# Attention bias with a mask, added by accumulating DMAs instead of by GpSimd, in a three-stage decoder layer; another order of steps

## The reference

```
x = x + attn(ln(x))            # stage a: 8 heads of 128, one shared key/value head, causal
x = x + xattn(ln(x), ctx, bias, pad, mask)   # stage b: 16 heads of 16
x = x + ffn(ln(x))             # stage c: shared expert + 8 experts, top 2 by a gate

# xattn, per batch and head
scores = q @ k.T * scale + mask          # mask: [256, 256], one for all batches
scores = where(pad, -inf, scores)        # pad: [32, 256]
scores = scores + bias + bias            # bias: [32, 16, 256, 256], the one large input
out    = softmax(scores) @ v
```

## Time and profile before

| | us |
|---|---|
| median of 3 runs (2559.65 to 2561.14) | 2559.83 |
| profiled execution | 2559.14 |
| its span, first to last instruction | 2557.4 |
| busy in it: TensorE, ScalarE, VectorE, GpSimd | 2340.5, 2060.2, 2007.8, 1788.1 |
| granted TensorE clock, mean | 0.991 |
| DMA queues' packets, share of the 16 engines | 27.4% |

### The profile page before, as it was taken

The page is one execution under the profiler, slowest core; times in us unless marked ns, Lnnn a source line. Parts: engine busy times, 40 slices in busy tenths (PEclk is TensorE's granted clock), DMA queues, the critical chain, the costliest instruction groups (busy, mean ns, idle before and its releaser), DMA issues.

```text
span 2557.4 us, 77106 instructions
## 1 busy us (share of the span) xinstructions
PE 2340.5 (92%) x26176; PEld 2036.7 (80%) x26176; DVE 2007.8 (79%) x6672; ACT 2060.2 (81%) x6065; POOL 1788.1 (70%) x1899
## 2 busy tenths in 40 slices
PE   4789999999999999999999999999999999999987
PEld 3678888888888888888888888888888888888876
DVE  5578788778788778788778788778788778788765
ACT  6777888877888877888877888877889877889864
POOL 2566677866677866677866677866677766677764
PEclk9899999999999999999999999999999999999999
DMA  5232222232222232222232222232222232222230
GB/s 167 92 105 87 92 86 89 84 109 86 92 88 89 84 109 82 96 87 90 84 109 81 96 86 91 85 109 80 94 87 93 84 109 80 93 88 93 80 100 10
DMA packets 171126, 233.14 MB, mean 91 GB/s; under 512 B 20720, under 2 KB 119280, under 8 KB 170736
## 3 DMA queue, kind: packets, MB, share of 16 engines
q1 hardware_dynamic: 170736, 228.21, 27.4%
HBM read 202.98 MB, written 25.17 MB: 89 GB/s over the span
## 4 chain that ended last, share of the span: by engine, by line
PE 63%; DVE 13%; ACT 11%; issue 10%; POOL 3%; DMA 1%; SPq 0%; DVEq 0%; ACTq 0%; POOLq 0%
PE ps_c_out L955 10%; PE ps_c_hidden L955 10%; PE ps_a_misc L955 9%; PE ps_b_probsT L1083 8%; PE ps_b_misc L1097 3%; PE ps_b_misc L955 3%; PE ps_b_scores L1071 3%; PE ps_a_scores L1009 3%; PE ps_a_misc L1028 2%; DVE b_neg_scores L817 2%; POOL bias L510 2%; DVE a_qT L769 2%; PE ps_b_probsT L955 2%; PE ps_b_scores L955 2%; PE ps_a_probsT L1016 1%
## 5 line engine op out<-in xcount | busy, mean ns | idle before, releaser
L510 POOL TENSOR_TENSOR bias<-bias,b_mask 128x512 f32<-128x512 f32 x512 | 646.9, 1278 | 0.0
L817 DVE CUSTOM_DVE_ANT_0 b_neg_scores<-ps_b_scores,bias 128x256 f32<-128x256 f32 x1024 | 391.7, 419 | 95.3 <-PE ps_b_scores L1071 34.8
L531 POOL TENSOR_TENSOR c_hidden_lo<-c_hidden,c_hidden_hi 128x512 f16<-128x512 f32 x288 | 334.2, 1160 | 131.2 <-ACT c_hidden_hi L683 90.8
L825 DVE TENSOR_TENSOR b_probsT_lo<-ps_b_probsT,b_probsT_hi 128x512 f16<-128x512 f32 x512 | 352.7, 689 | 63.6 <-ACT b_probsT_hi L660 53.7
L1083 PE MATMUL ps_b_probsT<-constants,b_probs 128*128 128x128 f32 x2048 | 323.3, 281 | 29.1 <-DVE b_probsT_lo L825 15.1
L524 POOL TENSOR_TENSOR c_hidden<-c_relu 128x512 f32<-128x512 f32 x288 | 300.3, 1043 | 56.3 <-ACT c_relu L678 55.2
L660 ACT ACTIVATE b_probsT_hi<-ps_b_probsT 128x512 f16<-128x512 f32 x512 | 303.1, 592 | 24.8 <-PE ps_b_probsT L1083 20.0
L955 PE MATMUL ps_c_out<-w_hi,c_hidden_hi 128*128 128x256 f16 x1152 | 314.3, 273 | 5.0 <-DVE acc L926 2.7
L955 PE MATMUL ps_c_hidden<-c_xT_hi,w_hi 128*128 128x256 f16 x1152 | 314.6, 273 | 3.7 <-ACT c_relu L678 2.3
L955 PE MATMUL ps_c_hidden<-c_xT_hi,w_lo 128*128 128x256 f16 x1152 | 314.8, 273 | 0.0
L955 PE MATMUL ps_c_hidden<-c_xT_lo,w_hi 128*128 128x256 f16 x1152 | 314.7, 273 | 0.0
(11 more groups left out here) (198 smaller groups left out, 8333.5 us busy)
## 6 DMA issues: line engine op xcount, KB each, us to landing
bias<-in_bias SPq DMA_DIRECT2D x256, 512.0 KB, 3.5
q_stack<-qk_scratch SPq DMA_DIRECT2D x256, 64.0 KB, 2.4
x_ln<-in_x SPq DMA_DIRECT2D x32, 256.0 KB, 2.8
ctxT<-in_ctx SPq DMA_DIRECT2D x32, 256.0 KB, 3.6
x_res<-in_x SPq DMA_DIRECT2D x32, 256.0 KB, 4.0
qk_scratch<-b_kT_hi_lo SPq DMA_DIRECT2D x32, 256.0 KB, 2.3
k_stack_even<-qk_scratch SPq DMA_DIRECT2D x128, 64.0 KB, 2.4
k_stack_odd<-qk_scratch SPq DMA_DIRECT2D x128, 64.0 KB, 2.4
```

The costliest lines, as they stand in the source:

```text
L510: gp.tensor_tensor(part, part, b_mask[:, :], ALU.add).then_inc(b_c_ok, 1)
L531: gp.tensor_tensor(c_hl[:, u, :], c_h[:, :], c_hh[:, u, :], ALU.subtract).then_inc(c_h_ok, 1)
L817: last = dve.tensor_tensor_reduce(out=b_t[:, u, c, :], in0=ps_bs[:, c * T:(c + 1) * T], in1=bias[:, slot, at:at + T], scale=-2.0, scalar=3 ...
L825: dve.tensor_tensor(b_pTl[:, j % 2, :, :], ps_bpt[:, :].rearrange("p (c t) -> p c t", c=CT), b_pTh[:, j % 2, :, :], ALU.subtract).then_inc ...
```

## The change

The tile `b_mask` is no longer added by GpSimd. For each pair of heads SP first copies it, twice side by side, into the bias slot (`b_fill`), SBUF to SBUF; then GpSimd's own queue issues a DMA that loads the 512 KB of bias and adds them to what lies in the slot (`b_comb`, now per pair). VectorE waits for that DMA's semaphore. The fill waits until the slot's former pair has been read and until the batch's mask is there; the mask of a batch is made only after the fills of the batch before have landed. The five lists of steps are replaced by others, and the last lag goes from 3 to 4.

```diff
@@ SyncE @@
-            sp.wait_ge(s_lo, N_PIECES)
-            for p in range(SLOTS):
-                sp.dma_start(bias[:, p, :], bias_d[p]).then_inc(s_bias[p], 16)
...
-            def b_load(b, p):
-
-                sp.wait_ge(b_t_ok, after(b, BH, 2 * p + 2))
-                q = p + SLOTS
-                if q < PAIRS:
-                    sp.dma_start(bias[:, p % SLOTS, :], bias_d[b * PAIRS + q]).then_inc(s_bias[p % SLOTS], 16)
...
+            def b_fill(b, p):
+
+                if b == 0 and p < SLOTS:
+                    sp.wait_ge(s_lo, N_PIECES)
+                sp.wait_ge(b_m_ok, b + 1)
+                sp.wait_ge(b_t_ok, max(b * BH + 2 * (p - SLOTS) + 2, 0))
+                sp.dma_start(bias[:, p % SLOTS, :].rearrange("p (h n) -> p h n", h=2),
+                             b_mask[:, None, :].to_broadcast([P, 2, CT * T])).then_inc(s_fill[p % SLOTS], 16)
@@ GpSimd @@
-            def b_comb(b, j):
-
-                p = j // 2
+            def b_comb(b, p):
+
                 slot = p % SLOTS
-                if j == 0:
-                    gp.wait_ge(b_m_ok, after(b, 1, 1))
-                if j % 2 == 0:
-                    gp.wait_ge(s_bias[slot], after(b, 32, 16 * (p // SLOTS + 1)))
-                part = bias[:, slot, (j % 2) * 512:(j % 2) * 512 + 512]
-                gp.tensor_tensor(part, part, b_mask[:, :], ALU.add).then_inc(b_c_ok, 1)
+                gp.wait_ge(s_fill[slot], 16 * (2 * b + p // SLOTS + 1))
+                gp.dma_start(bias[:, slot, :], bias_d[b * PAIRS + p], accum_op=ALU.add).then_inc(s_bias[slot], 16)
@@ VectorE: b_mask_row, b_s @@
-                dve.wait_ge(b_c_ok, after(b, BH, 0))
+                if b > 0:
+                    for slot in range(SLOTS):
+                        dve.wait_ge(s_fill[slot], 16 * 2 * b)
...
-                dve.wait_ge(b_c_ok, after(b, BH, j + 1))
+                dve.wait_ge(s_bias[slot], 16 * (2 * b + j // 2 // SLOTS + 1))
@@ the lists, SyncE's as an example @@
-        b_store_q:0@2 b_stack_q:0@2 a_T:0@1 b_load:0@2 b_mask:0@2 b_load:1@2 b_load:2@2 b_load:3@2 b_split_q:0@2
+        b_fill:4@3 b_fill:5@3 b_fill:6@3 b_mask:0@3 a_ln:0@2 b_fill:7@3 b_fill:3@2 b_fill:1@2 b_store_k:0@2
...
-LAGS = 3
+LAGS = 4
```

More of the change, by code:

```diff
@@ L108 @@
[L108 to L117 removed]
+        c_lo:2@4 b_kv:0@2 c_f1:3@4 a_q:3@2 b_comb:4@3 b_res:0@3 c_lo:3@4 c_f1:4@4 b_comb:5@3 c_lo:4@4 c_f1:5@4
@@ L255, in build @@
         s_bias = [sem(f"bias_loaded{n}") for n in range(SLOTS)]
+        s_fill = [sem(f"mask_in_bias{n}") for n in range(SLOTS)]
         s_xln, s_xres, s_ctx = sem("x_ln_loaded"), sem("x_res_loaded"), sem("ctx_loaded")
```

77 lines of the change are left out of this document (36 added, 41 removed).

## The result

The changed kernel takes 2665.39 us (median of 4 runs, 2662.86 to 2667.68) against 2559.74 us of the kernel before in the same session. The ratio is 1.0417, with a 95% interval of 1.0401 to 1.0432: it is 4.2% slower, 106 us. The prediction said 2519 us, 2475 to 2600.

What follows compares the result with a forecast made beforehand. TensorE was taken to bound the batch period, with gaps where it waits for VectorE. Per batch 0.3 + 1.2 + 0.3 - 0.5 = 1.3 us won, times 31 = 40 us: 2519 us, range 2475 to 2600.

Steps and rivals of the forecast that it cites:

- The removed additions: GpSimd's 16 additions per batch: 0.3 us won from VectorE's bias wait, 1.2 from gate instructions held up by GpSimd.
- The issues: 8 DMA issues per batch on GpSimd replace 16 additions: 0.45 to 1.28 us each, cost on the path 0.
- The limit of 2.6 us: On GpSimd: an issue of 2.6 us or more would use up its 21 us of slack per batch.
- The order: New step lists around a_s:1, a_pv:0 and b_s:0: 0.3 us won per batch, bounds 1.3 lost and 1.3 won.
- The accumulating load: GpSimd's bias DMA after the fill: lands in 3.5 to 5.1 us, cost 0, bounds 0 and 1.6 per batch.
- The DMA load: DMA queue share: from 27.4% busy to 60% with the fills' writes and the loads counted twice.
- The store and the stack: Output store behind the query stack in SP's queue, 0.4 us of room: 0.5 us lost per batch, bounds 0 and 3.
- Rival 1: At b_s:0, DMA contention delays stage b's first heads: net 1.3 us lost per batch, 2600 us; chance 0.18.
- Rival 2: Accumulating DMA far slower than a load, 8 us to landing: +2 per batch, 2620 and beyond; chance 0.12.
- Rival 3: Gate instructions on VectorE mostly meet an idle port: 2.5 us won per batch, 2482 us; chance 0.20.
- Rival 4: Stalls only move, a_pv:0 waiting where a_s:1 did, gains lost to the store: 2560 within 5; chance 0.14.
- The signs named for after: Profile after: 75.3 us period, GpSimd down about 647 us, no 1.5 us wait at a_s:1, b_s:0 within 24 us of c_T.

Runs made afterwards that it cites:

- x12: The kernel before without GpSimd's 16 additions per batch and nothing in their place, mask left out; 2503.6 us.
- x5: The changed kernel's new order with plain bias loads issued from GpSimd, no fill and no accumulation, mask left out; 2544.9 us.
- x2: The changed kernel's orders on all engines, with loads by SP and additions by GpSimd as in the kernel before; 2576.3 us.
- x13: x5 with an addition of 32 columns of zeros on GpSimd behind each of its 8 issues per batch; 2554.0 us.
- x4: The changed kernel without the fills, accumulating loads kept, mask left out; 2590.8 us.
- x1: The changed kernel with the output store moved ahead of the next batch's fills and stores in SP's list; 2636.1 us.
- x3: The changed kernel with plain loads in place of accumulating ones, fills kept, mask left out of the result; 2606.9 us.
- x15: x3 with the output store first in SP's queue; 2532.8 us.
- x11: x9 with GpSimd's third bias addition also moved earlier, behind a_kT_lo; 2527.6 us.
- x8: x1 with fills 0 and 1 ahead of the key's store and accumulating loads 0 and 1 some 8 us earlier; 2622.9 us.
- x7: The kernel before with VectorE's first g_mask pair moved behind a_s:0 and the second piece beside its successor; 2605.8 us.
- x9: The kernel before with GpSimd's second bias addition moved directly behind the first; 2527.1 us.

## Why the prediction was wrong

**The removed additions (0.3 and 1.2 us per batch).** Right in mechanism, and the size was somewhat low: x12 measured 1.9. But the changed kernel doesn't get it. The five gate lines, `g_sum`'s included, take 195 us in the kernel before, 190 in the changed one, 88 in x5 and 131 in x12. A sixth line, the second `g_mask` pair, adds 12, 22, 49 and 14 us; the new order holds it where the old one didn't (52 us in x2). x13 shows what brings the hold back: 0.25 us more of GpSimd behind each issue puts GpSimd's other instructions back onto the gate. "Shrink as GpSimd's busy time there does, by 36%" was a wrong way to size it. What is held depends on which two instructions meet, not on a share of busy time.

**The issues (0.45 to 1.28 us each, cost 0).** The size was right, 0.885 us. The cost wasn't 0: a similar lengthening cost 9 us in x13, for the reason just given; the two intervals lie just apart. The limit of 2.6 us named for an issue left out the 20.4 us that the additions free; with them it would be twice that. That a gate instruction holds up a bias load shows in no row: the longest issue takes 1.22 us.

**The order (0.3 won, bounds 1.3 either way).** It lost 16 us, 0.5 per batch, by a wait for `a_qT_lo` that the prediction had not seen. The stall at `a_pv:0` for `a_qT`, which it had, came: 47.4 us. By x13 and x5 it comes with the held gate. That `b_s:0` would have 1.3 us more work ahead of it was counted; the waits for `b_probsT_lo`, which grew by 33 us, were not.

**The accumulating load (cost 0, bounds 0 and 1.6).** This and the next are the steps that failed. The time of all engines was bounded well, 1.6 to 3.2 us, and measured 3.0. The DMA load was well estimated too, 60% against 28.9 + 27.1 = 56% of a longer span. The landing was not: 6.9 us against at most 5.1 (5.8 without fills, x4). The prediction looked at this load's own time and its own reader, and charged 0 with a bound of 1.6 per batch. Accumulation measured 46 us without fills, 58 with them, and 103 with them and the store out of the way: 1.5, 1.9 and 3.3 per batch. Part of that lies with the load's own reader (70.7 us of VectorE's waits in x1, 10.5 in the changed kernel), part with the readers of what lands beside it, part with the gate and the clock.

**The store and the stack (0.5 us per batch, bounds 0 and 3).** The place was right and so was the room of 0.4 us. The store landed at 1300.8 instead of some 0.4 us ahead of its reader, for two reasons. Its 2.2 us to landing were taken from its old place in the queue; in the new place they are 4.8 with the old traffic (x2) and 6.0 in the changed kernel, 6.9 in the stretch above. And it was issued later: 7.0 us after the stack's first issue, where the prediction counted 5.3 and x2 has 5.1. In the version with plain loads the late store is worth 74 us (x3 less x15), 2.4 per batch against the 0.5 charged for it and the stack together, though within the bound of 3. With the store ahead of them the fills cost little beside plain loads, which is nearly what the prediction had.

Sum by steps: the prediction had +1.5 won, 0.3 won and 0.5 lost per batch. Measured along the path x2, x5, x3, changed kernel: 0.5 lost, 1.0 won, 2.0 lost, 1.9 lost, 3.4 us lost per batch.

**The rivals.** Rival 1, contention at the first heads, is what happened. Its threshold was a stack 2.7 us late; it was 3.7 late in the median. Its price of 2600 was 65 us too low. It priced one wait, TensorE's for the stack, and that one is no larger here than in x5; the store's wait, `b_neg_max` behind it and the bias loads' came beside it. Rival 2's number, 2620 and beyond, was nearer, but the load didn't take 8 us in the median. Rival 3, a gate that runs free, came in no run: with the additions gone and nothing added, x12 won 1.9 us per batch and not the 2.5 that this rival priced. Rival 4, stalls that only move, is seen in x11, x13 and x8.

**The clock.** No term of the sum had it, since it was at 1.0 in the whole steady part of the kernel before. The changed kernel lacks 44 us of clock, x3 36, x1 27 and x15 10. How many of the changed kernel's 106 us that makes isn't measured. In x7, 49 us of lacking clock were worth 18; by the same share it would be some 16 here, an estimate. TensorE's busy time points the same way: it grew by 32 us in x7 and by 30 here.

**The signs named for after.** The period (75.3) was wrong at 79.8. GpSimd's busy time fell by 393 us and not by 647, since the issues, 256 x 0.885 = 227 us, count in it, and instructions behind them grew. `g_mask` had a spread, with a median of 0.90 us against 1.04. The 1.5 us at `a_s:1` were gone, with no wait for `a_neg_max` over 1.0, but the wait at `a_pv:0` wasn't smaller, 1.57 us. `b_s:0` came 25.7 us after `c_T`, past the 24 named as the limit, and waited for the stack; `acc` waited for the store. The bias loads landed later than the 5 us named as a sign of failure. These were the right places to look.

**Open.** How the 103 us of accumulation in x1 divide among the late bias loads, the gate, the stack and the clock wasn't separated. TensorE is idle 72 us more in x1 than in x15 and busy 33 us more. x5 with the store first is missing. No version with masks by DMA came out below the kernel before.

## What to carry to other kernels

Price a new transfer by what it does to the landing of everything issued near it, and take those landings from a busy stretch. A reader with 0.4 us of room is lost when a landing goes from 2 to 6 us. A new place in the queue, with nothing added, was enough to take one from 2.2 to 4.8 us. Before work is moved off GpSimd to free VectorE, look for the pair of instructions that meet: one entry of an order (x9) won 34 us, more than half of the 58 that leaving out all 512 additions gives. And treat a wait of TensorE as possibly more than its length, since the clock behind it can fall; look at the granted clock before and after an edit.
